# VectorE masks the hidden layer right behind the row maxima; GpSimd takes the whole root, a low part and one split of queries and maxima; ScalarE writes the choice ahead of the joining

## The reference

```
x = x + tanh(g_xattn) * attention(Q=layernorm(x), K=ctx, V=ctx)   # 16 heads of 16, causal
x = x + tanh(g_ffn)   * ffn(layernorm(x))
ffn: prob = softmax(x @ w_router + b_router) over 16 blocks; the 4 largest are chosen
     h = relu(x @ w1^T + b1) (1024 wide, 16 blocks of 64), blocks not chosen are zeroed
     y = h @ w2^T + b2
```

## Time and profile before

| what | value |
|---|---|
| median of 3 executions | 723.73 us (722.40 to 725.18) |
| profiled execution, device time | 723.54 us |
| its span in the profile | 721.8 us |
| granted clock of TensorE, mean over the span | 0.986 of full speed |
| busy: PE, PEld | 686.2 us (95%), 628.9 us (87%) |
| busy: DVE, ACT, POOL | 576.3 us (80%), 514.2 us (71%), 512.2 us (71%) |
| instructions | 30666 |

### The profile page before, as it was taken

The page is one execution under the profiler, slowest core; times in us unless marked ns, Lnnn a source line. Parts: engine busy times, 40 slices in busy tenths (PEclk is TensorE's granted clock), DMA queues, the critical chain, the costliest instruction groups (busy, mean ns, idle before and its releaser), DMA issues.

```text
span 721.8 us, 30666 instructions
## 1 busy us (share of the span) xinstructions
PE 686.2 (95%) x13072; PEld 628.9 (87%) x13072; DVE 576.3 (80%) x1614; ACT 514.2 (71%) x785; POOL 512.2 (71%) x651
## 2 busy tenths in 40 slices
PE   6869999999999999999999999999999999999888
PEld 5657889998999999889899998989989899899787
DVE  5789988888887888888788888879888888977562
ACT  3656787787777778778777877877787786787532
POOL 3676767778777777877877787777777777765542
PEclk8979999999999999999999999999999999999999
DMA  5313354454345435435544443553454345242010
GB/s 163 99 42 61 75 109 87 86 109 91 77 98 108 89 87 108 86 70 109 108 80 95 109 75 88 102 109 76 98 105 74 88 109 87 59 79 47 20 37 30
DMA packets 161815, 61.91 MB, mean 86 GB/s; under 512 B 135696, under 2 KB 161424, under 8 KB 161680
## 3 DMA queue, kind: packets, MB, share of 16 engines
q1 hardware_dynamic: 160848, 58.38, 38.8%
q10 hardware_dynamic: 832, 1.57, 0.7%
HBM read 19.03 MB, written 8.39 MB: 38 GB/s over the span
## 4 chain that ended last, share of the span: by engine, by line
PE 61%; DVE 24%; issue 5%; ACT 4%; DMA 3%; POOL 2%; SPq 1%; POOLq 0%; ACTq 0%; DVEq 0%
PE bank L414 8%; PE bank L437 6%; PE score_banks L335 6%; PE bank L439 6%; PE bank L438 6%; PE bank L415 6%; PE bank L416 6%; PE score_banks L305 5%; PE bank L348 4%; DVE max_found_in L638 4%; PE bank L362 3%; DVE stats L608 3%; DVE hid L711 2%; DVE q_parts L651 2%; DVE x L666 2%
## 5 line engine op out<-in xcount | busy, mean ns | idle before, releaser
L832 POOL TENSOR_TENSOR h_low<-hid,h_high 128x512 fp32r<-128x512 f32 x128 | 165.2, 1291 | 118.6 <-ACT hid L532 118.4
L825 POOL TENSOR_SCALAR_AFFINE_SELECT weights<-weights 128x1024 f32<-128x1024 f32 x128 | 139.7, 1115 | 56.6 <-ACT weights L510 56.6
L414 PE MATMUL bank<-xT_high,w_high 128*128 128x256 f32 x496 | 151.1, 305 | 8.7 <-DVE hid L711 8.1
L510 ACT ACTIVATE weights<-score_banks 128x1024 f32<-128x1024 f32 x128 | 124.3, 1024 | 45.3 <-PE score_banks L335 45.3
L437 PE MATMUL bank<-w_high,h_high 128*128 128x256 f32 x488 | 142.0, 291 | 4.9 <-DVE y_out L689 4.3
L415 PE MATMUL bank<-xT_low,w_high 128*128 128x256 f32 x496 | 138.8, 280 | 0.0
L416 PE MATMUL bank<-xT_high,w_low 128*128 128x256 f32 x496 | 138.6, 279 | 0.0
L711 DVE SCALAR_TENSOR_TENSOR hid<-bank,b_cols,used_all 128x256 f32<-128x256 f32 x248 | 108.2, 477 | 36.9 <-PE bank L416 36.2
L439 PE MATMUL bank<-w_high,h_low 128*128 128x256 f32 x488 | 136.4, 280 | 0.0
L438 PE MATMUL bank<-w_low,h_high 128*128 128x256 f32 x488 | 136.3, 279 | 0.0
L414 PEld LDWEIGHTS bank<-xT_high,w_high 128*128 128x128 f32 x496 | 93.4, 188 | 19.4 <-DVE hid L711 14.0
(11 more groups left out here) (106 smaller groups left out, 1485.8 us busy)
## 6 DMA issues: line engine op xcount, KB each, us to landing
x_in<-in_x SPq DMA_DIRECT2D x31, 256.0 KB, 3.1
out_y<-y_out SPq DMA_DIRECT2D x31, 256.0 KB, 2.5
c_in<-in_ctx SPq DMA_DIRECT2D x30, 256.0 KB, 3.1
qT<-qT SPq DMA_DIRECT2D x128, 4.0 KB
w_stage<-in_w1T ACTq DMA_DIRECT2D x1, 1024.0 KB, 5.2
hid<-in_w2T SPq DMA_DIRECT2D x8, 128.0 KB, 2.6
kT_parts<-k_parts SPq DMA_TRANSPOSE x57, 3.3
qT_parts<-q_parts SPq DMA_TRANSPOSE x57, 3.3
```

The source lines that it names most:

```text
L414: pe.matmul(out=bank, lhsT=w1_high[:, k, c], rhs=high, start=k == 0, stop=False)
L510: act.activation(weights[:, b % 2, half * 2 * HB:(half + 1) * 2 * HB, :].rearrange("p h q -> p (h q)"), score_banks[:, 2 * half:2 * half + ...
L825: pool.affine_select(out=w, in_=w, compare_op=ALU.is_ge, fill=0.0, base=0, pattern=[[0, 2 * HB], [1, S]], channel_multiplier=-1).then_inc( ...
L832: pool.tensor_tensor(h_low[:, p % 2, chunks], hid[:, n % 4], h_high[:, p % 2, chunks].bitcast(F32), ALU.subtract).then_inc(h_low_made, 1)
```

## The change

Five things are written in another order or given to another engine.

1. VectorE's loop: `finished` stands ahead of `attention_added`, and `hidden_masked(p, m)` directly behind `row_maximum`, ahead of `normalised_again` and `layernorm_stats`.
2. Variance plus epsilon (L612, twice in an iteration) is computed by GpSimd, in front of the power.
3. `maximum_parts` is gone: `row_maximum` always writes its maxima into the padded queries of the tile that carries them, and GpSimd's `query_parts` copies queries, levels and maxima in one (21 columns of each head's 32 in place of 16), and so waits for `max_found`. It runs for two more tiles at the end, which have no queries and only carry maxima. The three memsets of `q_parts`' levels fall away.
4. GpSimd's loop: `query_parts` stands ahead of `values` and `key_parts`; the low part of a piece m+1 is made in the next iteration, behind `x2_b2` and ahead of `query_parts`.
5. ScalarE's loop: `choice` stands ahead of `q_joined`.

```diff
@@ scalar engine's loop
                 if p is not None:
                     hidden_parts(p, m)
+                if pr is not None:
+                    choice(pr)
                 if QUERIES_BY_PE <= i + 3 < N + MAX_LAG:
                     q_joined(i + 3)
-                if pr is not None:
-                    choice(pr)
@@ vector engine's functions
-            def stats_of(source, stats, mv, ve, s, b, stats_made, mean_made, ve_made):
+            def stats_of(source, stats, mv, s, b, stats_made, mean_made):
                 dve.bn_stats(stats[:, s, :], source).then_inc(stats_made, 1)
                 dve.wait_ge(stats_made, b + 1)
                 dve.bn_aggr(mv[:, s, :], stats[:, s, :]).then_inc(mean_made, 1)
-                dve.wait_ge(mean_made, b + 1)
-                dve.tensor_scalar(ve[:, s], mv[:, s, 1:2], LN_EPS, None, ALU.add).then_inc(ve_made, 1)
...
                 carrier = b + MAX_LAG
-                ride = q_pad[:, carrier % QS, :, RIDE_COL] if q_early(carrier) else max_found_in[:]
-                ride = ride.rearrange("p (t g u) -> p u t g", g=2, u=U)
+                if carrier >= N:
+                    dve.wait_ge(q_parts_made, carrier - QS - QUERIES_BY_PE + 1)
+                ride = q_pad[:, carrier % QS, :, RIDE_COL].rearrange("p (t g u) -> p u t g", g=2, u=U)
...
-            def maximum_parts(b):
...
-                dve.tensor_copy(q_parts[:, slot, :, :, RIDE_COL],
-                                max_found_in[:].bitcast(U16).rearrange("p (h l) -> p l h", l=2)).then_inc(max_parts_made, 1)
@@ vector engine's loop
+                if 0 <= i - OUT_LAG - 1 < N:
+                    finished(i - OUT_LAG - 1)
                 if 0 <= i - 2 < N:
                     attention_added(i - 2)
-                if 0 <= i - OUT_LAG - 1 < N:
-                    finished(i - OUT_LAG - 1)
                 if 0 <= i + 1 < N:
                     row_maximum(i + 1)
-                    if not q_early(i + 1 + MAX_LAG):
-                        maximum_parts(i + 1)
+                if p is not None:
+                    hidden_masked(p, m)
                 if 0 <= i - 2 < N:
                     normalised_again(i - 2)
                 if 0 <= i + 4 < N:
                     layernorm_stats(i + 4)
-                if p is not None:
-                    hidden_masked(p, m)
@@ gpsimd
-            def rstd_of(ve, result, s, b, ve_made, rstd_made):
+            def rstd_of(mv, ve, result, s, b, mean_made, ve_made, rstd_made):
+                pool.wait_ge(mean_made, b + 1)
+                pool.tensor_scalar(ve[:, s], mv[:, s, 1:2], LN_EPS, None, ALU.add).then_inc(ve_made, 1)
                 pool.wait_ge(ve_made, b + 1)
...
             def query_parts(b):
                 n, slot = divmod(b - QUERIES_BY_PE, 2)
-                pool.wait_ge(qn_made, b + 1)
+                if b < N:
+                    pool.wait_ge(qn_made, b + 1)
+                pool.wait_ge(max_found, b - MAX_LAG + 1)
                 if n >= 1:
                     pool.wait_ge(q_spread[slot], 16 * n)
-                pool.tensor_copy(q_parts[:, slot, :, :, 0:HD],
-                                 q_pad[:, b % QS, :, 0:HD].bitcast(U16).rearrange("p h (d l) -> p l h d", l=2)
+                pool.tensor_copy(q_parts[:, slot, :, :, 0:RIDE_COL + 1],
+                                 q_pad[:, b % QS, :, 0:RIDE_COL + 1].bitcast(U16).rearrange("p h (d l) -> p l h d", l=2)
                                  ).then_inc(q_parts_made, 1)
...
+                last_p, last_m = hidden_pair(i - 1)
+                if last_p is not None:
+                    hidden_low(last_p, last_m + 1)
+                if QUERIES_BY_PE <= i + 3 < N + MAX_LAG:
+                    query_parts(i + 3)
                 if i == FIRST:
                     values(0)
                 elif 0 < i + 3 < N:
                     values(i + 3)
-                if QUERIES_BY_PE <= i + 3 < N:
-                    query_parts(i + 3)
                 if KEYS_BY_PE <= i + 3 < N:
                     key_parts(i + 3)
...
                 if p is not None:
                     hidden_low(p, m)
-                    hidden_low(p, m + 1)
```

34 lines of the change are left out of this document (10 added, 24 removed).

## The result

Four runs of the changed kernel gave 698.5, 700.15, 700.8 and 703.63 us, a median of 700.47; beside them the kernel before had a median of 724.14. The ratio is 0.968, with a 95% interval of 0.9638 to 0.9721. The forecast was 704.5 in a range of 699 to 718. The profiled execution of the changed kernel took 700.15 us.

The account below looks back on a forecast made before the run. TensorE, in flight 95% of the span, was taken as the bound, so only its waits pay. Periods 13.5, end 3.5 and filling 2.0 us sum to 19.0, taking 723.54 to 704.5 us, range 699 to 718.

Parts of the forecast that it names:

- the periods: 27 two-iteration periods in the middle: 16.2 us of TensorE waiting goes, less 2.7 for thin cover and hold-ups, leaving 13.5.
- The floor of the period: Last middle period, 20.53 us against 21.13, taken as free of TensorE waits, so each normal period holds 0.60 us of waiting.
- `y_out` costs nothing: VectorE idles 0.70 us before the attention's chain, so `y_out`, 0.40 us, placed there first was costed at nothing.
- The mask 2.4 us earlier with 1.9 to spare: VectorE's mask directly behind the maxima ends at 311.3, TensorE wants it at 313.18; the whole 11.5 us wait goes.
- The choice ahead, 1.2 us for the maxima's row: SyncE's queue: the maxima's row starts 1.2 us earlier, against TensorE waits of at most 0.7 us, so that wait goes.
- `ve` and the halves on GpSimd: `ve` taken as 0.21 us, wider copy 0.20 more; GpSimd reaches 8.5 us an iteration, at worst 9.2, of 10.27, hidden.
- The thin cover of 0.5 us: Maxima's row lands by 321.6, TensorE's shifted scores due about 322.1: the plan's thinnest margin.
- the first rival: Thin cover fails through longer DMAs, each period keeps 0.3 us, the gain is about half: 712.5 us; chance 0.20.
- `q_pad` stays where it was: VectorE's `q_pad` stays at 313.94, as the first layernorm's power on GpSimd ends at 313.9.
- The end and the filling: Gains outside the periods: end 3.5 us (bounds 2 and 4.9) from `y_out` waits, filling 2.0 (0 and 3) from mask waits.
- Another loop holds the period: Rival: maxima, split, transposing DMA, joining and maxima's row keep the period at 21.13; only ends gain, 719.5 us; chance 0.10.
- GpSimd holds VectorE: Rival: GpSimd slows `xn`, `q_pad` and `x2`, VectorE needs 11.0 us an iteration, 741.5 us; sign turns at 2.7; chance 0.08.

Follow-up runs that it names:

- a_address: Changed kernel plus one unused tile of 64 bytes a partition, with no instruction different: 697.66 us, ratio 0.9639 to the kernel before.
- b_choice: Kernel before with only ScalarE's choice written ahead of the joining: 722.53 us, ratio 0.9986.
- b_mask: Kernel before with only the mask of the first hidden piece moved right behind the maxima: 714.12 us, ratio 0.9875.
- b_y_first: Kernel before with only `y_out` put at the head of VectorE's iteration: 715.67 us, ratio 0.9886.
- b_orders: Kernel before with mask, `y_out` and choice all moved; `ve` and halves stay on VectorE, GpSimd keeps its old order: 700.45 us, ratio 0.9687.
- c_pool_order: b_orders plus GpSimd's new order (low part and query split ahead of values and keys); `ve` and halves stay on VectorE: 695.90 us, ratio 0.9601.
- a_mask_late: Changed kernel with the mask put back behind `xn` and the second statistics: 699.75 us, ratio 0.9659 to the kernel before.
- a_choice_late: Changed kernel with the joining written ahead of the choice again: 707.12 us, ratio 0.9766 to the kernel before.
- a_ve_vector: Changed kernel with variance plus epsilon (`ve`) back on VectorE: 699.45 us, ratio 0.9646 to the kernel before.
- a_halves_vector: Changed kernel with the maxima's halves back on VectorE through a 64-byte tile, GpSimd's copy narrow again: 699.81 us, ratio 0.9651 to the kernel before.
- a_y_late: Changed kernel with `y_out` put back behind the attention's addition: 703.11 us, ratio 0.97 to the kernel before.

## Why the prediction was right, and where it was off

The sum was 19.0 us and 23.4 were measured (723.54 less 700.15, profiled executions; the spans differ by 23.8). The side, the range and the mechanism held. The largest term, the periods, was mis-sized: 13.5 for 18.5. That the range held owes something to luck. The median lies 1.5 us above its lower end of 699, and 2.8 us of it are an effect of addresses that the prediction did not know; a_address, the same kernel without that effect, took 697.66 and would have been below the range.

**The floor of the period** is the step that was wrong: "The last of them ... takes 20.53 us; there TensorE waits for nobody." TensorE did wait there. In the kernel before, the output layer's first matmul and the one behind it stand so in TensorE's order of time, and the same matmul once more half a period later:

```profile
309.28 0.36 PE L437 MATMUL bank<-w_high,h_high 128*128 128x256 f32 x1
309.48 0.28 PE L438 MATMUL bank<-w_low,h_high 128*128 128x256 f32 x1
...
319.91 0.39 PE L437 MATMUL bank<-w_high,h_high 128*128 128x256 f32 x1
```

The bank's first matmul lasts 0.36 or 0.39 us in place of 0.28. VectorE's `y_out`, which reads such a bank, started at 308.72 and took 0.48, so it ended at 309.20, just ahead of the matmul's 309.28. The matmul was issued while those ahead of it were still in flight, and so its wait is no idle time, and no view of waits names it. The two excesses, 0.08 and 0.11 us, are one period's, and make 0.19 of the 0.20 by which my floor was too high. The experiments agree: in the 27 periods 54 matmuls of L437, two a period, take over 0.33 us in the kernel before, in b_choice and in b_mask, and none in b_y_first and in b_orders, where `y_out` comes first (the longest is 0.28). Clean periods are 20.54 in b_mask and 20.34 in b_orders. By the floor of 20.33 that c_pool_order shows, the period held 0.80 us of waiting, and not 0.60: 21.6 us over 27. The changed kernel gives 2.6 of it back by addresses (26 periods of 20.43 in place of 20.33) and 0.5 by its one late period, which leaves the 18.5 measured. My 13.5 was 5.0 too small: 5.4 by the floor and 2.7 for hold-ups that hardly came, less these 3.1.

**`y_out` costs nothing.** Right: in the changed kernel it starts at 297.70, and VectorE's `gain` starts at 298.14, 0.04 us behind the end of TensorE's transposes at 298.10.

**The mask 2.4 us earlier with 1.9 to spare.** Right in size, with 1.7 to spare. But a_mask_late shows that the move was not needed within the whole. The prediction credited the 11.5 us to the mask's move; the other moves ahead of it on VectorE's queue (0.52 us by `y_out` and `ve`, the halves' 0.51 us and more) are enough by themselves.

**The choice ahead, 1.2 us for the maxima's row.** Right: the row starts directly behind the joining, and its waits fell from 5.8 to 0.2 us. a_choice_late prices it at 6.6 us within the change and b_choice at nothing outside it.

**`ve` and the halves on GpSimd.** Their groups, over the whole span of the changed kernel:

```profile
L624 DVE TENSOR_SCALAR q_pad<-x_in,mv,rstd 128x256 f32<-128x256 f32 x64 | 58.4, 912 | 46.1 <-POOL rstd L778 46.1
L804 POOL COPY q_parts<-q_pad 128x672 uint16<-128x672 uint16 x57 | 45.8, 804 | 0.0
...
L659 DVE TENSOR_SCALAR xn<-x,mv,rstd 128x256 f32<-128x256 f32 x64 | 41.8, 653 | 2.3 <-POOL rstd L778 2.2
...
L776 POOL TENSOR_SCALAR ve<-mv 128x1 f32<-128x1 f32 x128 | 30.0, 234 | 90.3 <-DVE mv L607 90.3
```

`ve` takes 234 ns (I took 210), 1.5 times VectorE's 154; a factor of two, which the prediction also tried, is one for two inputs, and `ve` has one tensor as input. The larger copy takes 804 (849), and GpSimd still waits 90.3 us for VectorE, so it is no bound: its 471.62 us over 54 iterations are 8.73 of 10.22 (8.5 forecast, 9.2 at worst). The move of `ve` gave nothing that a_ve_vector could tell. That of the halves gave nothing in the periods with the tile in its place (20.34 in a_address, 20.32 in a_halves_vector). The medians, 697.66 and 699.81, differ by 2.1 us and their ranges overlap; the fillings, 87.92 and 90.88, had granted clocks of 0.90 and 0.87, so a gain there is not shown. What counts on GpSimd is the order: b_orders and c_pool_order differ by 4.6 us by the medians, and by 6.1 us in the periods of their profiled executions (554.93 less 548.80).

**The thin cover of 0.5 us.** From the end of the attention's transposes to the end of the split passed 5.93 us before and pass 5.66 now, 0.27 earlier where I had 0.5. The joining starts 9.94 us behind them in place of 10.55. The cover held: the shifted scores waited once for the maxima's row in the middle, 0.2 us, and the first rival did not occur. In b_orders they waited nine times, 4.6 us in all.

**`q_pad` stays where it was.** Wrong, and without a price. It ends 8.82 us behind the end of the transposes in place of 7.69, and so fills the 1.1 us that were idle ahead of the next mask; that mask starts 8.74 behind them, in place of 8.80.

**The end and the filling.** 3.55 us for 3.5 and 1.74 for 2.0. The second is no confirmation: b_choice, whose edit should do nothing there, filled in 86.38 us at a clock of 0.92, so no run shows what the change does to the filling. a_y_late shows that `y_out`'s place makes 2.55 of the end. There the wait for `y_out` is 3.5 us, and when it goes a wait for `xn` is laid bare, as supposed. That wait, in the last 59 us of the changed kernel:

```profile
PEld bank L370 <- DVE xn L659: 1.2, 1, 1.2
```

**The rivals.** "Another loop holds the period" is out: no period stayed at 21.13. "GpSimd holds VectorE" is out as to the time but right as a mechanism. `q_pad` takes 912 ns on average and VectorE idles 46.1 us ahead of it, and `xn` takes 653 ns, or 1354 in a_mask_late. Above the undisturbed 0.41 us the hold-ups are 0.50 and 0.24 us an iteration. But the kernel before had part of them: means of 581 ns for `q_pad` and 667 for `xn`, so only 0.33 and nothing are new, far from the 2.7 that would decide it. And they lie where nothing is due: VectorE has 456.51 / 54 = 8.45 us of work in 10.22. The rule that I cited from the Trainium skill (GPSIMD Engine Reference, Key points: contention with VectorE's instructions in a two-port mode or with two SBUF inputs) is consistent with these rows: the maxima at 299.97 and the mask at 301.96, which read PSUM, kept their 1.20 and 0.88 us beside GpSimd's `x_b` and low part, and the SBUF-to-SBUF `q_pad` did not. It isn't proven by them: `xn` at 302.75, SBUF to SBUF as well, kept its 0.41 us beside the low part and the copy, and no trace shows in which mode an instruction runs.

What stays open: which tile's place sets TensorE's distance of 117 or 118 ns, what the change does to the filling, and whether c_pool_order's remaining lead of 1.8 us on a_address (695.90 and 697.66, with overlapping intervals) is real.

## What to carry to other kernels

Where two waits take turns in a loop, the trace's totals are not prices: each edit alone gave 0 to 10 us, the three together 24, and within the whole the most valuable one was the one that gave nothing alone. Take a period's floor from the matmuls' own durations and not from a period in which no wait is named, since a first matmul of 0.36 in place of 0.28 us is a wait too. And when an edit removes or adds a tile, compare the distance of identical matmuls before crediting or blaming the instructions it moved.

## What the runs showed of the hardware that was not expected

TensorE's pace depends on where tiles lie. With an unused tile of 64 bytes a partition kept in its place, the identical instructions of the hidden and output layers ran at other distances. The groups of the output layer from 90 to 630 us in the changed kernel, and then in a_address:

```profile
L436 PE MATMUL bank<-w_high,h_low 128*128 128x256 f32 x424 | 119.9, 283 | 0.0
L435 PE MATMUL bank<-w_low,h_high 128*128 128x256 f32 x424 | 119.5, 282 | 0.0
L434 PE MATMUL bank<-w_high,h_high 128*128 128x256 f32 x424 | 119.1, 281 | 0.0
```

```profile
L437 PE MATMUL bank<-w_high,h_low 128*128 128x256 f32 x424 | 118.7, 280 | 0.0
L436 PE MATMUL bank<-w_low,h_high 128*128 128x256 f32 x424 | 118.6, 280 | 0.0
L435 PE MATMUL bank<-w_high,h_high 128*128 128x256 f32 x424 | 118.5, 279 | 0.0
```

The means (the last figure but one) differ by 2 to 3 ns, about 1%, but in over 1,200 matmuls of the output layer here, and as many of the hidden one, and together it is worth 2.8 us of 700, as much as `y_out`'s place or the low part's within the change. The second thing is how little a held-up VectorE matters: in a_mask_late its mean `xn` is 3.3 times as long as undisturbed, and the kernel is as fast as any other that lacks the tile.
